# Rows and x1 fetched ahead between the phases of a mixture-of-experts and attention kernel, loops over experts written out, and finer semaphores

## The reference, cut to what matters

```python
def reference(X, Wq, Wk, Wv, Wc, Ltri, Wr, W1, W3, W2):     # X: (4, 2048, 256), T = 8192 tokens, 8 experts
    x = X
    x = x + 0.5 * ffn(layernorm(x), Wr, W1, W3, W2)
    x = x + attention(layernorm(x), Wq, Wk, Wv, Wc, Ltri)
    x = x + 0.5 * ffn(layernorm(x), Wr, W1, W3, W2)
    return x

def ffn(x, Wr, W1, W3, W2):                  # top 2 of 8 experts, at most 2560 tokens in one
    logits = clip(x @ Wr)
    top_v, top_i = top_k(logits, 2); top_p = softmax(top_v)
    xe = rows of the tokens of each expert, in their order, cut at 2560
    h = silu(xe @ W1) * (xe @ W3)            # W1, W3: 256 x 1024
    ye = h @ W2                              # W2: 1024 x 256
    return sum over a token's two experts of top_p * ye (nothing where it was cut)

def attention(x, ...):                       # 16 heads of 16, causal, without softmax
    KVc = cumsum(K outer V); Y = Q . KVc; Y = Bm Y; return Y @ Wc.T
```

## Time and profile before

| | |
|---|---|
| three runs | 3110.91, 3111.99, 3113.55 us (median 3111.99) |
| the profiled execution | 3110.48 us, of which the span from first to last instruction is 3108.8 us |
| PE busy | 2926.3 us (94%) |
| DVE, ACT, POOL busy | 1595.9 (51%), 1316.0 (42%), 1167.4 us (38%) |
| mean granted TensorE clock | 0.957 of full |
| chain that ended last | PE 35%, issue 1%, POOL 1%, DVE 1% of the span; the rest not told |
| route phase | 0 to 183 us |
| first expert phase | 183 to 1372 us |
| attention phase | 1372 to 1909 us |
| second expert phase | 1909 to 3109 us |

### The profile page before, as it was taken

How to read it: one execution, slowest core, us unless ns; L and a number is a source line. 1 busy time by engine, 2 the same in 40 slices (tenths; PEclk the granted TensorE clock), 3 DMA queues, 4 the chain that set the end, 5 groups by cost and what they waited for, 6 DMA issues and landing times. The chain is left out here.

```text
span 3108.8 us, 54843 instructions
## 1 busy us (share of the span) xinstructions
PE 2926.3 (94%) x18714; PEld 2615.2 (84%) x18714; DVE 1595.9 (51%) x3911; ACT 1316.0 (42%) x2807; POOL 1167.4 (38%) x1566
## 2 busy tenths in 40 slices
PE   6759999999999999969999994999999999999997
PEld 5758988989898989858888884898898988898986
DVE  7834544444544545426777774445445444445443
ACT  4633434343444434324554553434434343434433
POOL 3853434434444434320211122443434443443432
PEclk7569999999999999989999996999999999999999
DMA  7443323232323232120112013323233222323221
GB/s 258 141 105 62 70 41 81 40 77 40 77 41 75 48 67 41 30 60 29 43 56 70 29 43 91 83 41 75 50 64 78 42 54 56 78 40 75 41 35 26
DMA packets 156446, 198.43 MB, mean 64 GB/s; under 512 B 15600, under 2 KB 128368, under 8 KB 156272
## 3 DMA queue, kind: packets, MB, share of 16 engines
q0 software_dynamic: 64128, 88.42, 17.6%
q1 hardware_dynamic: 81856, 97.30, 10.1%
q10 hardware_dynamic: 10288, 10.38, 1.0%
HBM read 115.93 MB, written 80.11 MB: 63 GB/s over the span
## 5 line engine op out<-in xcount | busy, mean ns | idle before, releaser
L1106 DVE TENSOR_TENSOR e_h_lo<-e_hid,e_h_hi 128x384 fp32r<-128x384 f32 (+1 forms) x640 | 383.6, 599 | 399.0 <-ACT e_h_hi L1068 399.0
L1103 DVE TENSOR_TENSOR e_hid<-e_ps,e_gate 128x384 f32<-128x384 f32 (+1 forms) x640 | 381.6, 596 | 341.9 <-ACT e_gate L1064 341.7
L1068 ACT ACTIVATE e_h_hi<-e_hid 128x384 fp32r<-128x384 f32 (+1 forms) x640 | 356.7, 557 | 431.7 <-DVE e_hid L1103 430.4
L1064 ACT ACTIVATE e_gate<-e_ps 128x384 f32<-128x384 f32 (+1 forms) x640 | 333.4, 521 | 351.2 <-PE e_ps L88 351.0
L86 PE MATMUL e_ps<-e_xT_hi,c_wa 128*128 128x384 f32 (+1 forms) x1280 | 457.6, 357 | 18.6 <-DVE e_hid L1103 11.8
L86 PE MATMUL e_ps<-e_xT_hi,e_wb 128*128 128x384 f32 (+1 forms) x1280 | 466.5, 364 | 2.2 <-DVE e_yrow L1116 1.9
L88 PE MATMUL e_ps<-e_xT_hi,e_wb 128*128 128x384 f32 (+1 forms) x1280 | 456.5, 357 | 0.0
L87 PE MATMUL e_ps<-e_xT_lo,e_wb 128*128 128x384 f32 (+1 forms) x1280 | 456.1, 356 | 0.0
L88 PE MATMUL e_ps<-e_xT_hi,c_wa 128*128 128x384 f32 (+1 forms) x1280 | 452.0, 353 | 0.0
L87 PE MATMUL e_ps<-e_xT_lo,c_wa 128*128 128x384 f32 (+1 forms) x1280 | 452.0, 353 | 0.0
L920 POOL DMA_INDIRECT e_xrow<-normed_rows,e_token x328 | 357.3, 1089 | 181.9 <-issue 141.7
(11 more groups left out here) (293 smaller groups left out, 5382.6 us busy)
## 6 DMA issues: line engine op xcount, KB each, us to landing
raw<-w SPq DMA_DIRECT2D x204, 256.0 KB, 3.1
normed_rows<-r_xn SPq DMA_DIRECT2D x8, 1056.0 KB, 5.5
normed_rows<-mi_xn SPq DMA_DIRECT2D x8, 1056.0 KB, 4.8
r_xin<-x SPq DMA_DIRECT2D x8, 1024.0 KB, 8.2
x<-r_xin ACTq DMA_DIRECT2D x8, 1024.0 KB, 5.1
mi_x<-x SPq DMA_DIRECT2D x8, 1024.0 KB, 8.0
out<-mi_x SPq DMA_DIRECT2D x8, 1024.0 KB, 5.3
e_xrow<-normed_rows,e_token POOLq DMA_INDIRECT x328, 2.9
```

What stands on the lines that cost most here:

```text
L1064: act.activation(gate[:, f % 2, 0:n], ps1[f % 2][:, 0:n], ACT.Silu).then_inc(gated, 1)
L1068: act.activation(h[0][:, f, 0:n], hid[:, f % 2, 0:n], ACT.Copy).then_inc(h_high, 1)
L1103: dve.tensor_tensor(hid[:, f % 2, 0:n], ps3[f % 2][:, 0:n], gate[:, f % 2, 0:n], ALU.mult).then_inc(hid_ready, 1)
L1106: dve.tensor_tensor(h[1][:, f, 0:n], hid[:, f % 2, 0:n], h[0][:, f, 0:n].bitcast(F32), ALU.subtract).then_inc(h_ready, 1)
```

## The change

`raw` and the gathered rows `xrow` now live through the whole program. Four columns of rows are gathered by POOL at the end of the route phase and of the attention phase, as soon as the slot table is written (`slots_ready`); in the expert phases POOL's tile gathers the rows of the tile behind it as its last step, with where that begins computed on POOL, which now loops over 8 experts with one written out. At the end of the first expert phase SP, once all additions have landed, loads the first group of `x1` in four parts with a semaphore each, and two whole groups, into `raw`. ACT and DVE have the 8 experts written out. PE's block `f = 1` waits for the lent banks alone (`y_lent_kept`), and `y_kept` is waited for before the second product. Each of the 12 weight pieces has its semaphore, and SP issues all 12 without waiting between them; the route phase no longer waits for expert 1's pieces at its end.

```diff
...
+        dve.tensor_tensor(token[:, 0:SCOLS], self.tokenf[:], self.unfilled[:], ALU.add).then_inc(self.slots_ready, 1)
...
+class Ahead:
...
+    def gather(self, pool, xn, token, phase):
+        for sub in range(BIG):
+            pool.indirect_dma_start(
+                self.xrow[:, sub, :], None, xn, bass.IndirectOffsetOnAxis(ap=token[:, sub:sub + 1], axis=0),
+                bounds_check=ROWS - 1, oob_is_err=True).then_inc(self.rows_loaded[phase], 16)
+
+    def load_x1(self, sp, x1, x1_g):
+        for i in range(MG // 2):
+            sp.dma_start(x1[:, 0, 2 * i:2 * i + 2], x1_g[0][:, 2 * i:2 * i + 2]).then_inc(self.x_first[i], 16)
+        for g in (1, 2):
+            sp.dma_start(x1[:, g], x1_g[g]).then_inc(self.x_loaded[g], 16)
...
-        wait(sp, raw_loaded[q % 2], 16 * (PIECES // 2 * n + q // 2))
...
-        sp.dma_start(dst, src).then_inc(raw_loaded[q % 2], 16)
+        sp.dma_start(dst, src).then_inc(raw_loaded[q], 16)
...
-                load_expert(sp, w, 1, raw, raw_loaded, 1)
+                load_expert(sp, w, 1, raw, raw_loaded)
...
-                wait_raw(sp, raw_loaded, 1)
...
+                pool.wait_ge(cleared, 16 * 3)
+                for i in range(2):
+                    pool.wait_ge(xn_stored[i], 16 * (GR // 2))
+                pool.wait_ge(r.slots_ready, 1)
+                ahead.gather(pool, xn_out, slot_token, 0)
...
+        def counts(eng, e):
+            return (eng.value_load(table.first[0:1, bass.ds(e, 1)], min_val=0, max_val=E * MAX_TILES),
+                    eng.value_load(table.big[0:1, bass.ds(e, 1)], min_val=1, max_val=MAX_BIG),
+                    eng.value_load(table.small[0:1, bass.ds(e, 1)], min_val=1, max_val=MAX_SMALL))
...
+                if phase == 0:
+                    sp.wait_ge(w_low, PIECES * (E + 1))
+                    sp.wait_ge(all_added, 1)
+                    ahead.load_x1(sp, rows_of(raw), groups_of(acc))
...
-                def gather(g):
-                    wait_alone(pool, next_held, g + 1, k.passed)
-                    for sub in range(BIG):
-                        pool.indirect_dma_start(
-                            xrow[:, sub, :], None, xn,
-                            bass.IndirectOffsetOnAxis(ap=token[:, sub:sub + 1], axis=0),
-                            bounds_check=ROWS - 1, oob_is_err=True).then_inc(x_loaded, 16)
+                def gather(at, g):
+
+                    wait_alone(pool, x_turned, KD * g + 2 * KD, k.passed)
+                    pool.tensor_copy(token[:], slot_token[:, bass.ds(at, BIG)]).then_inc(token_ready, 1)
+                    wait_alone(pool, token_ready, g + 1, k.passed)
+                    wait_alone(pool, next_held, g + 2, k.passed)
+                    ahead.gather(pool, xn, token, phase)
...
-                def tile(e, s, subs, first, at, g):
-                    wait_alone(pool, x_turned, KD * g + KD, k.passed)
-                    pool.tensor_copy(token[:], slot_token[:, bass.ds(at, BIG)]).then_inc(token_ready, 1)
-                    wait_alone(pool, token_ready, g + 1, k.passed)
-                    gather(g)
+                def tile(e, subs, at, behind, g):
                     meta(g)
                     hold(e, subs, at, g)
                     wait_alone(pool, y_kept, g + 1, k.passed)
                     add(BIG)
+                    gather(behind, g)
+
+                def expert(e):
+
+
+                    f, big, small = counts(pool, e)
+                    at = e * UPE
+                    tile(e, SMALL, at, pool.snap(at + SMALL), f)
+                    with pool.Fori(0, big) as t:
+                        own = pool.snap(at + SMALL + t * BIG)
+                        tile(e, BIG, own, pool.snap(own + BIG), pool.snap(f + 1 + t))
+                    number = pool.snap(f + 1 + big)
+                    at_small = pool.snap(at + SMALL + big * BIG)
+                    rest = pool.snap(at + UPE - at_small - small * SMALL)
+                    with pool.Fori(0, small) as t:
+                        own = pool.snap(at_small + t * SMALL)
+                        last = pool.snap((t - small + MAX_SMALL + 1) // MAX_SMALL)
+                        behind = nc.s_assert_within(
+                            own + SMALL + last * rest, 0, SCOLS,
+                            skip_runtime_bounds_check_because="counts are clamped: a column behind a tile, or the region's end")
+                        tile(e, SMALL, own, pool.snap(behind), pool.snap(number + t))
...
-                experts(pool, tile)
+                with pool.Fori(0, E) as e:
+                    expert(e)
 
                 n = total(pool)
-                wait_alone(pool, x_turned, KD * n + KD, k.passed)
-                gather(n)
                 meta(n)
...
+                pool.nop().then_inc(all_added, 1)
...
-                            pe.wait_ge(y_kept, g + 2)
+                            pe.wait_ge(y_lent_kept, g + 1)
...
                     turn(WORDS * g + 2 * WORDS)
+                    pe.wait_ge(y_kept, g + 2)
...
-                experts(act, tile)
+                for e in range(E):
+                    expert(act, tile, e, e % 2)
...
+                dve.nop().then_inc(y_lent_kept, 1)
...
+                        if sub == 2:
+                            ins.then_inc(y_lent_kept, 1)
...
-                experts(dve, tile)
...
+                for e in range(E):
+                    expert(dve, tile, e, e % 2)
...
-        x1 = m.sb("x1", [P, 3, MG, D])
+        x1 = rows_of(raw)
...
+        def wait_x1(eng, g, c):
+
+            if g == 0:
+                if c % 2 == 0:
+                    eng.wait_ge(x_first[c // 2], 16)
+            elif c == 0:
+                eng.wait_ge(x_loaded[g % 3], 16 * (g // 3 + (g % 3 != 0)))
...
-                for g in range(3):
-                    load(g)
...
+                for b in range(2):
+                    pool.wait_ge(xn2_stored[b], 16 * (MGS // 2))
+                pool.wait_ge(r.slots_ready, 1)
+                ahead.gather(pool, xn_out, slot_token, 1)
...
-                    if c == 0:
-                        dve.wait_ge(x_loaded[g % 3], 16 * (g // 3 + 1))
+                    wait_x1(dve, g, c)
...
-        raw_loaded = [m.sem(f"raw_loaded{b}") for b in range(2)]
+        raw_loaded = [m.sem(f"raw_loaded{q}") for q in range(PIECES)]
...
-        with ExitStack() as early:
-            raw = early.enter_context(nc.sbuf_tensor("raw1", [P, WCOLS], F32))
...
-        middle_phase(nc, k, x1, xn, out, slot_token, tiles[1])
-        with ExitStack() as late:
...
+        raw = m.sb("raw", [P, WCOLS])
+        ahead = Ahead(m)
+        route_phase(nc, k, attention, x, xn, x1, out, slot_token, weights, slot_a, raw, raw_loaded, ahead, tiles[0])
+        expert_phase(nc, k, "e1_", 0, xn, x1, slot_token, weights, slot_a, raw, raw_loaded, ahead, tiles[0], 2)
+        middle_phase(nc, k, x1, xn, out, slot_token, raw, ahead, tiles[1])
+        expert_phase(nc, k, "e2_", 1, xn, out, slot_token, weights, slot_a, raw, raw_loaded, ahead, tiles[1], 2 + E)
...
```

More of the change, by code:

```diff
@@ L469, in tiles, with __init__ @@
         dve.tensor_copy(table.first[:, 1:E + 1], scan)
+class Ahead:
+    def __init__(self, m):
+        self.xrow = m.sb("xrow", [P, BIG, DX])
+        self.rows_loaded = [m.sem(f"rows_loaded{i}") for i in range(2)]
+        self.x_first = [m.sem(f"x1_first{i}") for i in range(MG // 2)]
+        self.x_loaded = [m.sem(f"x1_loaded{b}") for b in range(3)]
+    def gather(self, pool, xn, token, phase):
[8 more added lines that the diff above has]
+            sp.dma_start(x1[:, g], x1_g[g]).then_inc(self.x_loaded[g], 16)
 class TileTable:
@@ L657, in load_expert, with route_phase @@
             dst = piece(raw, q).rearrange("p (k d) -> p k d", d=D)
-        sp.dma_start(dst, src).then_inc(raw_loaded[q % 2], 16)
+        sp.dma_start(dst, src).then_inc(raw_loaded[q], 16)
 def wait_raw(eng, raw_loaded, n, q=None):
     if q is None:
-        for b in range(2):
-            eng.wait_ge(raw_loaded[b], 16 * (PIECES // 2) * (n + 1))
-    else:
-        eng.wait_ge(raw_loaded[q % 2], 16 * (PIECES // 2 * n + q // 2 + 1))
-def route_phase(nc, k, attention, x_in, xn_out, x1_out, out, slot_token, w, slot_a, raw, raw_loaded, tiles_out):
+        for q in range(PIECES):
+            eng.wait_ge(raw_loaded[q], 16 * (n + 1))
+    else:
+        eng.wait_ge(raw_loaded[q], 16 * (n + 1))
+def route_phase(nc, k, attention, x_in, xn_out, x1_out, out, slot_token, w, slot_a, raw, raw_loaded, ahead,
+                tiles_out):
     with ExitStack() as ctx:
@@ L828, in _, with expert_phase @@
                 r.tabulate(pe, GR - 1, False, True, 2)
-def expert_phase(nc, k, name, xn, acc, slot_token, w, slot_a, raw, raw_loaded, table, loaded):
+def expert_phase(nc, k, name, phase, xn, acc, slot_token, w, slot_a, raw, raw_loaded, ahead, table, loaded):
     with ExitStack() as ctx:
@@ L848, in expert_phase @@
         y_weight = m.sb("y_weight", [P, BIG])
-        xrow = m.sb("xrow", [P, BIG, DX])
```

(19 more changed lines are left out.)

26 lines of the change are left out of this document (12 added, 14 removed).

## The result

The changed kernel takes 3072.6 us (median of four runs, 3070.87 to 3073.59) where the kernel before took 3111.7 us beside it (3110.91 to 3113.55). The ratio is 0.9873, with a 95% interval from 0.9856 to 0.989. Predicted were 3087 us in a range from 3071 to 3102; the gain is 39.1 us where 24.3 were worked out.

What follows compares the result with a forecast made beforehand. PE, busy 94% of the span, was taken as the bound, so only its idle time and pace could be won. 14.1 + 11.4 + 0.4 - 7.0 + 5.4 = 24.3 us gave 3087 us, own range 3081 to 3094, with rivals 3071 to 3102.

Steps and rivals of the forecast that it cites:

- The outer loops: Expert phases: writing out ACT's and DVE's loop over experts removes six stalls of PE behind `hid`, 14.1 us gained.
- The fourth rival: The loop's stall stays because reading counts makes it, not the return; only 3.9 us won, 3097 us, chance 0.08.
- The third: Rival: ACT's or DVE's longer streams stall on code fetch at inner loops or expert borders, up to 3141 us, chance 0.06.
- The lent banks: PE's block 1 in expert tiles: waiting for two of four scalings, not all, gains 11.4 us.
- The gather before the barrier: Ends of route and attention phases: barriers 4.3 and 11.75 us later; net +0.4 us first expert phase, -7.0 us second.
- the first rival: POOL's DRAIN costs nothing behind gathers, barriers come 5.7 us earlier in both places, 3076 us, chance 0.19.
- the prediction's three parts: POOL's chain behind the barrier: first gather gone 5.0 us, `hold`'s wait 0.9, lent banks 0.5; together given as 6.3 us.
- the low clock: Second tile of each expert phase: after PE stands some 5 us, a stretch at reduced clock costs 1.6 us.
- pieces without waits: Weight loads issued in a burst: conversion comes a tile later and POOL's 10 us cover a burst beside a gather; zero.
- one like the first: PE's hole before the second expert phase, taken to resemble the 22.64 us before the first gathered rows.
- x1 ahead: Start of the attention phase: SP loads `x1` before the barrier, so PE's transposes start earlier, 5.4 us gained.
- the address of `wb`: Odd experts' weight slot moves by 4,224 bytes with the same remainder to 128; put at zero.

Runs made afterwards that it cites:

- ACT's loop alone: The changed kernel with ACT's outer loop over four pairs of experts put back, DVE's experts still written out: 3086.77 us, ratio 0.9929 to the kernel before.
- that experiment: The kernel before with `xrow` allocated ahead of `wb`, moving the odd experts' weights 4,224 bytes, nothing else changed: 3106.76 us, ratio 0.999 to the kernel before.

## Why the prediction was right in direction and 14 us short

**The outer loops: right, 14.1 forecast, 16.8 measured.** The six entries gave 14.9 us in the trace of after, the eight others 1.9. ACT's return costs 0.8 to 1.0 us in the first phase and 3.9 to 4.1 in the second, and it comes back whole with ACT's loop alone. The fourth rival, that reading the counts makes the stall, is out: the counts are still read. The third, that longer streams stall elsewhere, is out too: no entry takes over 27.1 us. What makes the second phase's returns dear is in the trace: ACT is idle 2.1 to 2.4 us longer at each than in the first phase, with two instruction packets in that time and none in the first phase; the table load of 1.28 us is there in both. By the Trainium skill, "Runtime: NRT & Kernel Launch", § Instruction fetch mechanics, straight code is streamed, and a taken branch to a page that isn't held waits for its fetch. The trace agrees: these packets lie at the returns of the second phase, and at the borders of the changed kernel PE never waits behind `hid`.

**The lent banks: right, 11.4 forecast, 11.4 measured** by the kernel that takes them back, over the tiles between an expert phase's start and its last tile.

**The gather before the barrier: the step that failed.** The prediction has the sequence "the barrier then at 175.35 + 1.0 + 5.0 + 5.7 + 0.2". It took the 5.71 us of a DRAIN that closes a phase with hundreds of indirect DMAs and set it behind four gathers. Two things are wrong in that. After one or four gathers a DRAIN ended 2.0 us after the last one's work (once 3.1), 0.2 us after its landing where that is recorded; and its recorded length, in the first phase, counts from 176.54, before the gathers are done (180.44). Both places had the barrier 3.6 us earlier than forecast. That is part of the first rival (3076 us), not all of it: the DRAIN isn't free. By the Trainium skill, "VectorE: DVE Perf Modes", § The DRAIN you can't avoid, the DRAINs that the runtime puts at a kernel's start and end are constant at about 12 ns. Those of POOL that close a block here are not: 43 ns where POOL had long been idle, 53 ns behind another DRAIN, and 3.3 to 12.6 us for the first one after gathers or a whole phase; the measurement decides.

Behind the barrier the trace follows the steps. In the first phase POOL's chain came to 42.2 us from the memset (41.7 forecast, where the prediction's three parts, 5.0, 0.9 and 0.5, add to 6.4 us and not to its 6.3), and the low clock took 2.6 us, not 1.6: with the 3.6 us, 2.4 us gained where 0.4 were forecast. In the second it came to 45.7 us, not 43.2, because SP's burst of twelve pieces is issued just there: the term "pieces without waits", put at zero, costs 2.5 to 3 us at this one place. After its halt of 1.82 us the clock was full: 4.3 us lost where 7.0 were forecast. (The hole before the second phase's first rows, "one like the first" in the prediction, was 15.85 us long and not 22.64; no term rests on it.)

**x1 ahead: right, 5.4 forecast,** 6.3 by the hole before the phase and 5.7 by the kernel that undoes it.

**What was put at zero and wasn't: the address of `wb`.** "With the same remainder to 128; nothing": the profile of before showed blocks of 2.12 us with one weight slot and 2.08 with the other, and the move changed the slower one. By its trace it is 4.8 us, less 0.9 in the five tiles named at that experiment.

The failed steps come to 7.2 (barriers), 4.8 (address) and 2.7 (loops), and 0.9 at x1, less 2.5 and 0.5 for the chains, and with 1.6 less 1.0 for the clock; 1.3 us of the gain inside the phases went in tiles of 4 columns behind a first tile. That is 11.9 of the 13.6 us that the profiled executions differ from the forecast; the route phase's scatter has 1.2 of the rest.

The measured 3072.6 us lie in the stated range, from 3071 to 3102, by 1.6 us, and outside the prediction's own range from 3081. The range reached that low for the first rival alone, which gave 7.2 of its 11.4 us; that the address gave another 4.8 us was luck, and no part of the argument.

## What to carry to other kernels

Moving work ahead of a barrier moves the barrier too: compare what runs until then with the same work placed first behind it, which here was as good. A recorded length of a sequencer's instruction is not a price; its end, set against the end of the engine's work ahead of it, is. And when the same instruction runs at two paces from two buffers, ask for the buffers' addresses before putting a move of one at zero.

## What the runs showed of the hardware that was not expected

- POOL's DRAIN ended 1.9 to 2.1 us after the engine's last work behind one or four gathers (3.1 once), 6.4 to 6.7 us after it behind a whole expert phase of indirect DMAs; it lasted 5.5 to 5.7 us from its start when these had already landed, and 0.05 to 0.3 us when another DRAIN had gone before with up to three additions since. From how many DMAs it grows isn't known.
- The address of the weights, divided by 2,048 bytes, left the remainder 640 for `c_wa`, and 1,568, 1,696, 1,792 or 640 for `e_wb` in the four placements tried. A matmul of 512 columns started every 227 ns at 640 and every 232 to 233 ns at the other three; one of 384 columns every 173 ns at 640 and 1,696, and every 176 to 177 ns at 1,568 and 1,792. The moving operand had the same remainder throughout. Which part of the address counts isn't known.
- ACT's loop return made an entry 0.8 to 1.2 us longer in one phase and 3.1 to 5.1 us in the other, with the same instructions, and in the second phase its price moved by 1 us and more from one build to the next. ACT's idle time there was 3.5 to 3.8 us with two fetches of instructions in it, against 1.4 us without any.
- One addition of zeros, issued just as twelve loads of 256 KB were, landed 6.5 to 9.2 us after its issue; with two of those loads in flight, in the kernel before, it took 4.8 us, and in the first phase, with none beside it, 3.8 to 4.0.
